# Mixing stage of a hybrid block kernel: a batch's sums from GpSimd to VectorE, and a new order of the work around them

## The chip, the cores and the metric

One Trainium2 chip, one core of it. The metric is the device time of one launch in microseconds; lower is better. All arithmetic is fp32, with a few bf16 helpers for ranks and biases.

## The reference

The input x has 8 batches of 1024 tokens with 128 features. Four blocks follow each other, each reading the layer-normalised x and adding its result to x:

```
x = x + attention(layernorm(x))      # linear attention, 16 heads of 8, rotary, relu features
x = x + ffn(layernorm(x))            # 8 experts, the best 2 of each token, weights val
x = x + mixing(layernorm(x))         # a recurrence over the 1024 tokens of a batch, per feature
x = x + ffn(layernorm(x))            # the same experts and router again
```

The expert block ends in `y[m] = val[m,0] * result[m,0] + val[m,1] * result[m,1]`. The mixing block forms keys, values and a gate from x and from x shifted by one token. Per feature it keeps a numerator and a denominator that decay by exp(w), with the exponents taken against a running maximum. Its output is sigmoid(r) times the quotient, through one more matrix.

## The kernel before, in words

The two expert stages gather tokens into queues by expert in DRAM. Each batch is half `c = 0` and half `c = 1`, of four tiles of 128 tokens. GpSimd scatters a batch's normalised rows into `queue_dram` by 16 indirect DMAs (`scatter`, L547 to L560), with a small memset of a scratch tile between two of them in all but the last batch (`space`, L545). The experts run over tiles of 256 rows, and scatter results into `result_dram`.

Between the two expert stages lies the mixing stage, the one that the diff touches. It runs once per batch b = 1 to 8, in program order on each engine (b = 2 to 5 in a loop). Each engine's part is called `mixing`. Work of several batches is in hand at once:

- Batch b itself: VectorE multiplies values with exponentials (`weighted_values`), runs two scans (`states`, L1558 and L1559), forms the outputs (`outputs`, L1564 to L1575) and the quotient (`divided`, L1582). TensorE multiplies with the output matrix on top of the old x (L1139, L1145), and ScalarE copies the sum to `xres` (L901). SyncE stores it.
- Batch b+1: ScalarE normalises its x into `hmix` (`normalise`, L655), with the reciprocal deviations (`inverse_deviations`, L649) and VectorE's `shift` (`scales_in`, L1245). TensorE turns it (L935) and forms the keys (L1114, L1115). VectorE takes the running maximum (`maxima`, L1543) and the differences to it (`gaps`, L1548). ScalarE clamps these (`clamp_past`, L836) and exponentiates (`exponentials`, L842 to L848), where L848 also needs TensorE's gate product.
- Batch b+2: the results of the first expert stage come back to `back_x` (tile name `qkv`). ScalarE multiplies them with the gates (`weight`, `weigh`, L753, 16 instructions). Then GpSimd adds, for each half, x and the first result (L611) and the second result (L613): `sums` and `combine`. VectorE takes the moments of the sum (`way_in_moments`, L1233 and L1238), which batch b+2 needs when it is normalised one batch later.
- Batch b-1 on its way to the second expert stage: it is normalised into `hffn`, routed by TensorE, and VectorE picks its experts (`choose`, L1276 to L1294) and its places in the queues (`place`, L1300 to L1309). `place_ready` starts the GpSimd scatter number b+7.

The order on VectorE in a batch is: `weighted_values`, both scans, the two shifts, `outputs`, `maxima`, `divided`, `gaps`, `choose`, moments of `xres`, `place`, moments of the sum of b+2. On ScalarE: the deviations of b-1 and of b+1 and the normalising, `invert` (L855, L859), `weight(b+2)`, `clamp_past(b+1)`, the two `xres` copies, `exponentials(b+1)`. On GpSimd, the sums of batch b+2 stand between scatter b+6 and scatter b+7, and wait in program order behind the scatter of the batch before. Batches 7 and 8 form no sums, and batch 8 looks at no next batch. After it come the scatters 14, 15 and 16, the plan of the second expert stage and that stage.

The sums of the batches 1 and 2 are made by VectorE already, inside the end of the first expert stage (L1367 and L1369, with the same tile shapes).

Of the kernel before, what the change touches and what calls it, by code (L numbers as in the profile page):

```python
# [66 lines left out]
def program(nc, x, cosine, sine, consts, w_qkv, w_out, g_qk, g_qk_swapped, g_out, bias_cols, w_router,  # L67
            router_rows, w_up, w_down, up_bias, down_bias, channel, w_k, w_v, w_r, w_o, out):
    with ExitStack() as ctx:
# [468 lines left out]
        def _(pool):  # L538
# [66 lines left out]
            def combine(c, b, s):  # L605

                pool.wait_ge(x_loaded[c], b * 16 + 16 * BATCH)
                pool.wait_ge(weighted[c], b)
                y = back_x[c].rearrange("p (j k) d -> p j k d", k=TOPK)
                total = xsum[s][c]  # L610
                nc.gpsimd.tensor_tensor(total[:], xin[c][:], y[:, :, 0, :], ALU.add).then_inc(first_added[c], 1)  # L611
                pool.wait_ge(first_added[c], b)
                nc.gpsimd.tensor_tensor(total[:], total[:], y[:, :, 1, :], ALU.add).then_inc(xsum_ready[c], 1)  # L613

            def sums(b, s):
                for c in range(HALVES):
                    pool.wait_ge(summed[c], b - 2)
                    pool.sem_inc(place_taken, 1)
                    combine(c, b, s)

            sums(3, 1)
            with pool.Fori(0, 2) as n:
                sums(n * 2 + 4, 0)
                scatter(n * 2 + (1 + BATCH), 1)
                sums(n * 2 + 5, 1)
                scatter(n * 2 + (2 + BATCH), 0)
            sums(BATCH, 0)
# [5 lines left out]
        def _(act):  # L633
# [122 lines left out]
            def weight(m):  # L756

                take_gates(m)
                for c in range(HALVES):
                    weigh(c, m)  # L760
                act.wait_ge(weighted[HALVES - 1], m)

# [58 lines left out]
            def normalise_in(b, s):  # L821

                for c in range(HALVES):
                    inverse_deviations(c, b + BATCH, var_ready, moment, rstd, rstd_ready)
                for c in range(HALVES):
                    normalise(c, scale_ready, b, xsum[s], rstd, shift, hmix, h_ready)
# [51 lines left out]
            def mixing(b, s, before, routed=True, ahead=True, weighed=True):  # L878
# [4 lines left out]

                if routed:
                    deviations_routed(b - 1)
# [8 lines left out]
                if weighed:  # L894
                    weight(b + 2)
                if ahead:
                    clamp_past(b + 1)
                for c in range(HALVES):
                    act.wait_ge(mixed_ready[c], b)
                    act.wait_ge(x_stored[c], (b + BATCH) * 16)  # L900
                    nc.scalar.activation(xres[c][:], tiles4(ps_half[c]), ACT.Copy).then_inc(xres_ready[c], 1)  # L901
                if ahead:
                    exponentials(b + 1)
# [8 lines left out]
            experts(FIRST)  # L912
            normalise_in(1, 1)
# [281 lines left out]
        def _(dve):  # L1195
# [359 lines left out]
            def states(row):  # L1555

                dve.wait_ge(ev_ready, row)
                return (mark(nc.vector.tensor_tensor_scan(num[:, after], expo[:, 2, :], ev, num[:, 0:1], ALU.mult, ALU.add)),  # L1558
                        mark(nc.vector.tensor_tensor_scan(den[:, after], expo[:, 2, :], expo[:, 3, :], den[:, 0:1], ALU.mult, ALU.add)))  # L1559
# [24 lines left out]
            def mixing(b, s, before, routed=True, ahead=True, two_ahead=True):  # L1584
# [3 lines left out]
                scans = states(b)  # L1588
                if routed:
                    scales_for_experts(b + (BATCH - 1))  # L1590
                if ahead:
                    scales_in(b + (1 + BATCH))
# [6 lines left out]
                if routed:  # L1599
                    choose(b + (BATCH - 1), SECOND, 1 - s, before)  # L1600
                for c in both:
                    dve.wait_ge(xres_ready[c], b + BATCH)
                moments(xres, stats2, moment2, var2_ready)
                if routed:
                    place(b + (BATCH - 1), SECOND, 1 - s)
# [135 lines left out]
```

## Time and profile before

| | |
|---|---|
| median of 3 runs | 1095.58 us (1095.22 to 1096.97) |
| the profiled execution | 1094.39 us |
| its span in the trace | 1092.5 us |
| mixing stage in it | about 545 to 857 us |
| busy in the span | PE 805.5, POOL 748.8, DVE 708.1, ACT 573.4 us |
| granted TensorE clock, mean | 0.839 |

PE is TensorE, DVE is VectorE, ACT is ScalarE, POOL is GpSimd and SP is SyncE. Times in the trace are microseconds from the start of the span. The mixing stage is read batch by batch: the first `hmix` instruction (L655) of a batch on ScalarE is used as the mark of that batch. In a row of the timeline several instructions of one line stand as one, with their number behind an x.

### The profile page before, as it was taken

What the parts mean: (1) busy time and instruction counts of PE and PEld (TensorE: products, weight loads), DVE (VectorE), ACT (ScalarE), POOL (GpSimd) and SP (SyncE); (2) the same over time, 40 slices, a digit from 0 to 9 for tenths busy, and PEclk for the clock granted to TensorE, in tenths of its full rate; (3) what the DMA queues carried; (4) which work ended last, traced back from release to release, by engine and by line L of the source; (5) the groups of instructions that cost most, each with busy time, mean ns of one, the idle gap of its engine ahead of it and who ended that gap; (6) DMA issues with size and microseconds to landing.
All of it is one profiled execution on the core that took longest, in us unless ns stands there. A gap on an engine that the chain in (4) does not pass through costs nothing.

```text
span 1092.5 us, 19253 instructions
## 1 busy us (share of the span) xinstructions
PE 805.5 (74%) x4480; PEld 648.4 (59%) x4481; DVE 708.1 (65%) x2600; ACT 573.4 (52%) x1588; POOL 748.8 (69%) x1091
## 2 busy tenths in 40 slices
PE   3687787876419999999855676555751399999991
PEld 2466667765408999998623344323441399999881
DVE  4588898885524454454568888888854155666665
ACT  2786676662204434335578888888840143433430
POOL 2007776675755888887802589898888388888884
PEclk9788887786559999999878887778855699999996
DMA  7023222222245565566312231331114355789885
GB/s 197 20 59 88 82 77 66 87 73 70 80 130 159 178 189 184 184 189 197 102 58 77 87 111 38 102 104 51 54 59 129 85 181 186 240 265 293 282 248 158
DMA packets 159975, 142.67 MB, mean 131 GB/s; under 512 B 17539, under 2 KB 132876, under 8 KB 159792
## 3 DMA queue, kind: packets, MB, share of 16 engines
q1 hardware_dynamic: 121744, 70.98, 23.5%
q10 hardware_dynamic: 20448, 37.23, 10.5%
q0 software_dynamic: 17728, 33.88, 9.0%
q8 instruction: 16, 0.26, 0.1%
q14 instruction: 39, 0.32, 0.1%
HBM read 93.47 MB, written 50.37 MB: 132 GB/s over the span
## 4 chain that ended last, share of the span: by engine, by line
PE 41%; POOL 17%; DVE 14%; ACT 12%; issue 11%; DMA 3%; DVEq 0%; POOLq 0%; SPq 0%; ACTq 0%; another core or an unknown queue 0%
PE banks L1059 14%; POOL queue_dram L557 8%; PE banks L1079 7%; POOL result_dram L570 6%; PE banks L935 4%; POOL spacer L545 3%; PE banks L961 3%; DVE stats L1233 3%; PE banks L949 2%; ACT hmix L655 2%; PE banks L1067 2%; PE banks L1114 2%; ACT qkv L753 2%; PE banks L989 2%; PE banks L1115 2%
## 5 line engine op out<-in xcount | busy, mean ns | idle before, releaser
L557 POOL DMA_INDIRECT queue_dram<-hffn,place_i x256 | 297.5, 1162 | 169.8 <-remote 119.4
L570 POOL DMA_INDIRECT result_dram<-ytile,result_row x284 | 280.6, 988 | 93.1 <-issue 39.6
L1059 PE MATMUL banks<-xt,tile_up 128*128 128x256 f32 x1136 | 271.8, 383 | 5.2 <-DVE gated L1412 5.2
L769 ACT ACTIVATE gated<-banks,tile_bias 128x256 f32<-128x256 f32 x284 | 119.0, 470 | 234.4 <-PE banks L1059 196.0
L1412 DVE SCALAR_TENSOR_TENSOR gated<-banks,tile_bias,gated 128x256 f32<-128x256 f32 x284 | 124.2, 479 | 157.1 <-ACT gated L769 156.4
L1059 PEld LDWEIGHTS banks<-xt,tile_up 128*128 128x128 f32 x1136 | 207.1, 192 | 28.8 <-issue 3.6
L1079 PE MATMUL banks<-wdown_sb,gated 128*128 x1136 | 149.9, 275 | 3.9 <-DVE ytile L1420 3.9
L1079 PEld LDWEIGHTS banks<-wdown_sb,gated 128*128 128x128 f32 x1136 | 138.2, 192 | 4.5 <-issue 4.3
L545 POOL MEMSET spacer<- 128x176 f32 x508 | 138.8, 273 | 0.2
L935 PE MATMUL banks<-k_sb,hmix 128*128 128x128 f32 x128 | 30.0, 380 | 98.7 <-ACT hmix L655 69.9
L1067 PE MATMUL banks<-k_sb,xtile 128*128 128x128 f32 x284 | 55.4, 277 | 55.5 <-DMA xtile<-queue_dram 55.5
L935 PEld LDWEIGHTS banks<-k_sb,hmix 128*128 128x128 f32 x128 | 19.9, 192 | 110.4 <-ACT hmix L655 86.9
L1067 PEld LDWEIGHTS banks<-k_sb,xtile 128*128 128x128 f32 x284 | 40.2, 143 | 70.5 <-issue 55.1
L775 ACT ACTIVATE xt<-banks 128x256 f32<-128x256 f32 x142 | 54.5, 384 | 52.0 <-PE banks L1067 51.9
L1401 DVE SCALAR_TENSOR_TENSOR result_row<-xtile,expert_all 128x2 int32<-128x2 f32 x142 | 30.2, 213 | 64.8 <-DMA xtile<-queue_dram 42.9
L961 PE MATMUL banks<-wqkv_sb,hmix_t 128*128 128x384 f32 x128 | 57.8, 536 | 7.9 <-DMA bias_rows<-split_dram 7.4
L1114 PE MATMUL banks<-hseq,wnow_sb 128*128 128x512 f32 x96 | 60.0, 711 | 0.3
L1420 DVE TENSOR_TENSOR ytile<-banks,down_bias_sb 128x256 f32<-128x256 f32 x142 | 58.6, 413 | 0.0
L1115 PE MATMUL banks<-hseq,wpast_sb 128*128 128x512 f32 x96 | 55.9, 668 | 0.0
L668 ACT ACTIVATE qkv<-banks 128x384 f32<-128x384 f32 x64 | 31.2, 490 | 31.4 <-PE banks L940 31.4
L935 PE MATMUL banks<-k_sb,hffn 128*128 128x128 f32 x128 | 22.3, 314 | 33.0 <-ACT hffn L655 17.7
L935 PEld LDWEIGHTS banks<-k_sb,hffn 128*128 128x128 f32 x128 | 18.0, 165 | 46.2 <-issue 17.5
(213 smaller groups left out, 1579.7 us busy)
## 6 DMA issues: line engine op xcount, KB each, us to landing
tile_up<-w_up ACTq DMA_DIRECT2D x142, 256.0 KB
xtile<-queue_dram SPq DMA_DIRECT2D x142, 130.0 KB, 2.3
qkv<-result_dram SPq DMA_DIRECT2D x24, 512.0 KB, 5.4
x_dram<-xres SPq DMA_DIRECT2D x32, 256.0 KB, 2.8
result_dram<-ytile,result_row POOLq DMA_INDIRECT x284
xin<-x SPq DMA_DIRECT2D x16, 256.0 KB, 4.5
xold<-x SPq DMA_DIRECT2D x16, 256.0 KB, 4.1
queue_dram<-hffn,place_i POOLq DMA_INDIRECT x256, 2.4
```

The lines of the kernel that those rows point to most:

```text
L545: clear = nc.gpsimd.memset(spacer[:, slot, :], 0.0)
L557: nc.gpsimd.indirect_dma_start(queue_dram, bass.IndirectOffsetOnAxis(ap=place_i[s][:, at:at + 1], axis=0), hffn[s][c][:, j, :], None).then ...
L570: nc.gpsimd.indirect_dma_start(result_dram, bass.IndirectOffsetOnAxis(ap=result_row[i % SLOTS][:, h:h + 1], axis=0), ytile[i % SLOTS][:, h ...
L769: last = nc.scalar.activation(gated[i % GSLOTS][:, h, :], ps_up[i % 2][:, h, :], ACT.Silu, bias=tile_bias[i % STEP][:, h:h + 1])
L935: last = nc.tensor.transpose(dst[:, j * P:(j + 1) * P], src[:, j, 0:D], ident)
L961: nc.tensor.matmul(dst, hmix_t[c][:, j * P:(j + 1) * P], wqkv_sb[:], start=True, stop=False)
L1059: last = nc.tensor.matmul(ps_up[i % 2][:, h, :], tile_up[i % WSLOTS][:, h * P:(h + 1) * P], xt[i % 2][:], start=True, stop=True)
L1067: last = nc.tensor.transpose(ps_xt[i % 2][:, part * P:(part + 1) * P], xtile[i % SLOTS][:, part, 0:D], ident)
L1079: last = nc.tensor.matmul(y, gated[i % GSLOTS][:, h, tokens], wdown_sb[:, bass.ds(e * (HCH * D) + h * D, D)], start=(h == 0), stop=(h == H ...
L1114: nc.tensor.matmul(part, wnow_sb[:, i, :], hseq[:, 1 + c * CHUNK:1 + (c + 1) * CHUNK], start=True, stop=False)
L1115: last = nc.tensor.matmul(part, wpast_sb[:, i, :], hseq[:, c * CHUNK:(c + 1) * CHUNK], start=False, stop=True)
L1412: last = nc.vector.scalar_tensor_tensor(gated[i % GSLOTS][:, h, :], ps_up[i % 2][:, HCH + h, :], tile_bias[i % STEP][:, HCH + h:HCH + h + ...
```

## The change

The sums of the batches 3 to 8 go from GpSimd to VectorE. GpSimd only scatters in the mixing stage. VectorE forms the sum of half 0 after `choose`, then `place` (which stood behind the moments of `xres`), then the moments of `xres`, then the sum of half 1, then its moments. On ScalarE the weighing is split: half 0 before the `xres` copies, half 1 after them, and `clamp_past` behind both. ScalarE computes the deviations of b+1 ahead of those of b-1. VectorE computes the shifts between the two scans, those of b+1 first, and not behind both.

```diff
@@ gpsimd
-            def combine(c, b, s):
-                pool.wait_ge(x_loaded[c], b * 16 + 16 * BATCH)
-                pool.wait_ge(weighted[c], b)
-                y = back_x[c].rearrange("p (j k) d -> p j k d", k=TOPK)
-                total = xsum[s][c]
-                nc.gpsimd.tensor_tensor(total[:], xin[c][:], y[:, :, 0, :], ALU.add).then_inc(first_added[c], 1)
-                pool.wait_ge(first_added[c], b)
-                nc.gpsimd.tensor_tensor(total[:], total[:], y[:, :, 1, :], ALU.add).then_inc(xsum_ready[c], 1)
-            def sums(b, s):
-                for c in range(HALVES):
-                    pool.wait_ge(summed[c], b - 2)
-                    pool.sem_inc(place_taken, 1)
-                    combine(c, b, s)
-            sums(3, 1)
             with pool.Fori(0, 2) as n:
-                sums(n * 2 + 4, 0)
                 scatter(n * 2 + (1 + BATCH), 1)
-                sums(n * 2 + 5, 1)
                 scatter(n * 2 + (2 + BATCH), 0)
-            sums(BATCH, 0)
             for b in range(BATCH - 3, BATCH + 1):
                 scatter(b + BATCH, b % 2, spread=b < BATCH)
@@ scalar
+            def deviations_in(b):
                 for c in range(HALVES):
                     inverse_deviations(c, b + BATCH, var_ready, moment, rstd, rstd_ready)
+            def normalise_in(b, s):
                 for c in range(HALVES):
                     normalise(c, scale_ready, b, xsum[s], rstd, shift, hmix, h_ready)
@@ scalar, mixing
+                if ahead:
+                    deviations_in(b + 1)
                 if routed:
                     deviations_routed(b - 1)
...
                 invert(b)
                 if weighed:
-                    weight(b + 2)
-                if ahead:
-                    clamp_past(b + 1)
+                    take_gates(b + 2)
+                    weigh(0, b + 2)
                 for c in range(HALVES):
                     act.wait_ge(mixed_ready[c], b)
                     act.wait_ge(x_stored[c], (b + BATCH) * 16)
                     nc.scalar.activation(xres[c][:], tiles4(ps_half[c]), ACT.Copy).then_inc(xres_ready[c], 1)
+                if weighed:
+                    weigh(1, b + 2)
+                    act.wait_ge(weighted[HALVES - 1], b + 2)
+                if ahead:
+                    clamp_past(b + 1)
@@ vector
-            def states(row):
+            def states(row, between):
                 dve.wait_ge(ev_ready, row)
-                return (mark(nc.vector.tensor_tensor_scan(num[:, after], expo[:, 2, :], ev, num[:, 0:1], ALU.mult, ALU.add)),
-                        mark(nc.vector.tensor_tensor_scan(den[:, after], expo[:, 2, :], expo[:, 3, :], den[:, 0:1], ALU.mult, ALU.add)))
+                num_done = mark(nc.vector.tensor_tensor_scan(num[:, after], expo[:, 2, :], ev, num[:, 0:1], ALU.mult, ALU.add))
+                between()
+                return num_done, mark(nc.vector.tensor_tensor_scan(den[:, after], expo[:, 2, :], expo[:, 3, :], den[:, 0:1], ALU.mult, ALU.add))
@@ vector, mixing
-                scans = states(b)
-                if routed:
-                    scales_for_experts(b + (BATCH - 1))
-                if ahead:
-                    scales_in(b + (1 + BATCH))
+                def shifts():
+                    if ahead:
+                        scales_in(b + (1 + BATCH))
+                    if routed:
+                        scales_for_experts(b + (BATCH - 1))
+                scans = states(b, shifts)
...
                 if routed:
                     choose(b + (BATCH - 1), SECOND, 1 - s, before)
+                def next_sum(c):
+                    if two_ahead:
+                        dve.wait_ge(summed[c], b)
+                        combine(c, b + 2, s)
+                next_sum(0)
+                if routed:
+                    place(b + (BATCH - 1), SECOND, 1 - s)
                 for c in both:
                     dve.wait_ge(xres_ready[c], b + BATCH)
                 moments(xres, stats2, moment2, var2_ready)
-                if routed:
-                    place(b + (BATCH - 1), SECOND, 1 - s)
+                next_sum(1)
                 if two_ahead:
                     way_in_moments(b + 2, s)
```

## Rows read from the trace of the kernel before

**Rows 1.** Chain of waits, 530 to 870: start, duration, what

```profile
715.02 1.23 POOL xmid L611
...
856.47 2.29 DMA queue_dram<-hffn,place_i
```

**Rows 2.** Timeline of POOL: start, duration, instruction, [idle before, releaser]; first issues of scatters

```profile
755.59 0.99 POOL L557 DMA_INDIRECT queue_dram<-hffn,place_i  x1 [0.86 <-remote]
...
786.05 0.96 POOL L557 DMA_INDIRECT queue_dram<-hffn,place_i  x1 [2.25 <-remote]
...
815.30 0.96 POOL L557 DMA_INDIRECT queue_dram<-hffn,place_i  x1 [0.17 <-POOL spacer L545]
...
837.52 0.96 POOL L557 DMA_INDIRECT queue_dram<-hffn,place_i  x1 [0.17 <-issue]
```

**Rows 3.** Windows, queue_dram instructions: stretch, length, POOL busy, PEclk, DMA share, GB/s

```profile
721.11:749.43 28.32, 21.74 (x16) 0.76 0.24 76
```

**Rows 4.** Waits of ACT, 600 to 770: us in total, times, longest

```profile
ACT hmix L655 <- DVE shift L1245: 8.8, 4, 2.6
```

**Rows 5.** Timeline of ACT: hmix, invert and the last exponential of batches

```profile
593.08 3.19 ACT L655 ACTIVATE hmix<-xmid,shift,rstd 128x128 f32<-128x128 f32 x8
...
622.79 1.02 ACT L848 ACTIVATE rope_s<-banks 128x1024 f32<-128x1024 f32 x1 [1.37 <-PE banks L1115]
...
626.03 3.19 ACT L655 ACTIVATE hmix<-xold,shift,rstd 128x128 f32<-128x128 f32 x8
...
693.84 3.19 ACT L655 ACTIVATE hmix<-xold,shift,rstd 128x128 f32<-128x128 f32 x8 [1.70 <-DVE shift L1245]
...
705.38 1.14 ACT L855 ACTIVATE rope_c<-rope_c 128x512 f32<-128x512 f32 x2
...
722.90 1.01 ACT L848 ACTIVATE rope_s<-banks 128x1024 f32<-128x1024 f32 x1
...
728.50 3.19 ACT L655 ACTIVATE hmix<-xmid,shift,rstd 128x128 f32<-128x128 f32 x8 [2.42 <-DVE shift L1245]
...
762.99 3.19 ACT L655 ACTIVATE hmix<-xold,shift,rstd 128x128 f32<-128x128 f32 x8 [2.59 <-DVE shift L1245]
```

**Rows 6.** Timeline of DVE: the sum of one half, as VectorE already makes it

```profile
531.84 0.68 DVE L1367 TENSOR_TENSOR xold<-xin,qkv 128x512 f32<-128x512 f32 x1
532.56 0.69 DVE L1369 TENSOR_TENSOR xold<-xold,qkv 128x512 f32<-128x512 f32 x1
```

**Rows 7.** Timeline of DVE in the mixing stage, batches 4 to 7

```profile
678.98 2.06 DVE L1293 COPY hffn<-top_f 128x4 f32<-128x4 f32 x2
...
704.46 2.35 DVE L1543 TENSOR_TENSOR_SCAN top<-w_sb,top,banks 128x1024 f32<-128x1024 f32 x1 [3.65 <-PE banks L1115]
...
742.68 1.22 DVE L1548 TENSOR_TENSOR rotated<-banks,top 128x1024 f32<-128x1024 f32 x1
...
758.16 2.35 DVE L1558 TENSOR_TENSOR_SCAN num<-expo,num,rotated 128x1024 f32<-128x1024 f32 x1
...
778.13 0.23 DVE L1276 COPY hffn<-k_sb 128x4 f32<-128x4 f32 x2
...
781.77 1.64 DVE L1233 BATCH_NORM_STATS2 stats<-xres 128x6 f32<-128x128 f32 x8
...
783.87 0.23 DVE L1300 TENSOR_REDUCE seen_new<-member 128x8 f32<-128x64 bf16 x1
```

**Rows 8.** Timeline of PE: last rank product of batch 7

```profile
781.85 0.19 PE L1000 MATMUL banks<-seen,ones_bf 128*128 128x64 bf16 x1
```

**Rows 9.** Timelines of ACT and PE in batch 1

```profile
572.23 4.78 ACT L753 ACTIVATE qkv<-qkv,gate 128x128 f32<-128x128 f32 x16
...
578.38 1.16 PE L1145 MATMUL banks<-wo_sb,squares 128*128 128x128 f32 x8 [0.52 <-DVE squares L1582]
...
582.72 1.28 ACT L842 ACT_TABLE_LOAD   x1
```

**Rows 10.** Timeline of PE: turning a batch's hmix after an idle time

```profile
627.73 1.12 PE L935 MATMUL banks<-k_sb,hmix 128*128 128x128 f32 x4 [4.98 <-ACT hmix L655]
```

More of the change, by code:

```diff
@@ L754, in weigh @@
                 last.then_inc(weighted[c], 1)
[L756 to L761, printed above, removed]
             def experts(f):
@@ L818, in experts @@
                 steps(LAST, FINAL)
-            def normalise_in(b, s):
+            def deviations_in(b):
                 for c in range(HALVES):
                     inverse_deviations(c, b + BATCH, var_ready, moment, rstd, rstd_ready)
+            def normalise_in(b, s):
                 for c in range(HALVES):
@@ L912, in _ @@
             experts(FIRST)
+            deviations_in(1)
             normalise_in(1, 1)
```

## The prediction

> **What bounds the kernel now.** I read the chain of waits of the mixing stage first, because it says who is late. In its later batches it goes from the end of a scatter to the sum on POOL (L611), to VectorE's moments and scans, and to `hmix` on ScalarE; from batch 7 on it is POOL's scatters alone up to 856.47, when the last one starts [rows 1]. So two things set the end of the stage: when scatter 14 can start, and the three scatters 14 to 16 that follow it without a gap. Scatter 14 starts at 786.05, after POOL has been idle for 2.25 us: it waits for its places, not for POOL. Scatter 15 follows at 815.30 and scatter 16 at 837.52, each directly behind the one before [rows 2]. Nothing behind scatter 14 gets shorter, so the change is worth what it brings forward place 14.
>
> The timeline of ScalarE gives the pace. The `hmix` marks of the batches 5 and 6 are 34.66 us apart (693.84 and 728.50) [rows 5]. In the later batches ScalarE idles before `hmix` for VectorE's shift and, between two batches, for nothing else of a size that the change touches; these waits are 8.8 us over four batches [rows 4]. POOL's own load is a scatter of 28.3 us [rows 3] plus the sums, four instructions of the kind that took 1.23 us [rows 1]: scatter 13 starts 34.5 us after scatter 12 (721.11 and 755.59) [rows 2, 3]. So POOL and the chain through ScalarE and VectorE are about level now, and the change must relieve both.
>
> **Batches 3 to 6, ScalarE's path.** One batch is 11.54 us from `hmix` to `invert` (693.84 to 705.38), 18.53 us from there to the end of the last exponential (722.90 plus 1.01), and then a table load and four small roots. This last part took 2.22 us where nothing waited (622.79 plus 1.02 to 626.03), and 4.59 us where the shift was late (723.91 to 728.50) [rows 5]. After the change the deviations of b+1 come first and their shift stands between the scans, so it is no longer behind the second scan, of 2.27 us. ScalarE's own work stays the same: the split of the weighing reorders it. The new period is 11.54 + 18.53 + 2.22 = 32.3 us. I take the four shift waits as gone but for 0.05 us each (the shift's round trip lies beside the two later roots): 8.8 - 0.2 = **8.6 us** [rows 4].
>
> **Does VectorE fit?** From `hmix` to `gaps` is 14.18 us (728.50 to 742.68). Then follow `gaps` 1.14, `choose` 3.64 (778.13 to 781.77, in batch 7, where no sum of POOL lies beside it), the sum of half 0, `place`, the moments of `xres` 2.10 (781.77 to 783.87), the sum of half 1 and its moments 2.10 [rows 5, 7]. A half's sum took 0.72 + 0.69 = 1.41 us on VectorE, with scatters running on POOL [rows 6]. That is the nearest row, with the same shapes. `place` took 1.4 us, bounded by its first instruction at 783.87 and the scatter's start at 786.05 [rows 2, 7]. Adding 1.2 us for `weighted_values`, 2.3 for the first scan and 0.3 for the shifts: 14.18 + 1.14 + 3.64 + 1.41 + 1.4 + 2.10 + 1.41 + 2.10 + 1.2 + 2.3 + 0.3 = 31.2 us. This is under 32.3, so ScalarE sets the period, with a slack of 1.1 us on VectorE. The 2.8 us that the sums add are mostly paid by what goes: in batch 4 two copies of 128x4 took 2.06 us together, just when POOL's sum began, where the two of L1276 take 0.23 [rows 7], and where VectorE waits for `xres` now, `xres` comes earlier, ahead of the second half's weighing and the clamps.
>
> The second scan starts about 1 us later than now, because VectorE waits for the roots of b-1 between the scans. The cover is the wait for the keys before the running maximum, 3.65 us in batch 5 [rows 7], of which the earlier `hmix` takes 2 and the later scan 1; some 0.7 is left. If that cover is gone, VectorE's path grows by what is over. Behind the new waits of VectorE on `weighted` and `summed` the queue holds `place` and the moments; half 0 is weighed some 3 us before VectorE comes to it. SyncE's stores and loads wait for `xres` and the sums, which come within 2 us of their present times, and the results they load are used more than 20 us later: nothing.
>
> **Batch 1** has no scatter and no shift wait. VectorE's quotient of the second half lay beside a sum on POOL, and the output product that needs it came after an idle 0.52 us, at 578.38. I take that idle time as gone: it ends at some 578.8. ScalarE has weighed half 0 by 574.6 (572.23 plus half of 4.78), so it now waits for that product where it had other work. It copies `xres` until 579.4, weighs half 1 in 2.4 and clamps in 2.1 us: the table load comes at 583.9 and not at 582.72 [rows 9]. That is **1.2 us lost**. **Batch 2** has a wait of 1.37 us of the last exponential for TensorE [rows 5], whose ranks and value products stand behind `choose`, itself beside POOL's sum in this batch. It goes: **1.4 us gained**.
>
> **Batch 7** forms no sums. `place` moves ahead of the moments of `xres`: it started at 783.87, and can start when the ranks are there, at 782.1 [rows 7, 8]. That is **1.75 us** for scatter 14. Scatter 13 must be done by then. Place 13 comes 14.18 + 1.14 + 3.64 + 1.41 + 1.4 = 21.8 us after the `hmix` of batch 6, its scatter 0.9 us later, and it runs 28.3 us: it ends 51.0 us after that mark. Scatter 14 can start 32.3 + 20.5 + 0.9 - 0.1, some 53 us after it. So POOL is free by 2 us.
>
> **Sum:** 8.6 - 1.2 + 1.4 + 1.75 = 10.5 us (rounded). The profiled execution took 1094.39 us and so becomes 1083.9; the median shown is 1.2 above it, so the forecast against it is 1095.58 - 10.5 = **1085.1 us**. A measurement of this kernel can tell about 0.2%, 2.2 us.
>
> **Unknown costs.** A half's sum on VectorE beside a scatter: at best as above, at worst each of its two instructions waits for one scatter issue of 0.96 to 0.99 us [rows 2]. I take the measured 1.41. What a sum does to the scatter: at best nothing, at worst four instructions stretch it by their own time and one restart each, 4 x (0.69 + 0.5) = 4.8 us. I take 0.7. TensorE's idle time before a batch shrinks by some 2 us: no cost, and see (d).
>
> **Rivals.**
> (a) *VectorE becomes the bound, half-way.* If each instruction of a sum loses 0.5 us, VectorE's path is 33.2 us. Four periods of 33.2 against the present 137.0 (626.03 to 762.99) [rows 5] gain 4.2; with about 1 us less in batch 2 and place, some 5 us in all are left: 1090.5. For: only 1.1 us of slack, and the added wait between the scans. Against: VectorE's instructions kept their time beside scatters [rows 6].
> (b) *VectorE's sums queue behind POOL's issues: slower.* Each of four instructions waits 0.96 us, 3.84 in a batch. VectorE's path is 35.0 us; the batches 3 to 6 take 140.2 and not 137.0, so 3.2 lost; batch 1 loses 1.2, batch 2 1.5, the earlier place gives 1.75: 4.1 us slower, 1099.7. The point from which it is slower is 0.75 us per instruction. For: rows 7 show a small copy held for 2 us by POOL. Against: that was POOL's sum, not a scatter.
> The Trainium skill, "SBUF — State Buffer", section "SBUF: two separate sides", says that whichever of VectorE and GpSimd takes their common port pair first holds it for the whole instruction while the other blocks, and that a VectorE instruction with two SBUF inputs competes only with a GpSimd one that reads SBUF. If an issue counted as one, its price would be that of (b).
> (c) *POOL stays the bound.* Scatters of 28.3 + 4.8 us follow each other at 33.3 us and not 34.3: 4 us gained before scatter 14, 1091.3. For: in the trace the issues stretch beside VectorE's work, 21.74 us for 16 [rows 3] against 15.4 at 0.96 each [rows 2]. Against: it needs 3.7 us from the sums.
> (d) *TensorE's clock stays up.* Turning `hmix` takes 1.12 us for four at the low level. If the shorter idle time kept it high, some 2 us more would go per batch, until scatters bind: 1079. Against: after 4.98 us of idle it was already low [rows 10].
> (e) *No effect:* a wait not seen here holds ScalarE before `hmix`: about 1095.
>
> **How the numbers follow.** Forecast 0.68, (a) 0.12, (b) 0.05, (c) 0.07, (d) 0.04, (e) 0.04. The forecast's own range is 1082 to 1088.5. The range reaches over (a) and up to (c): 1080.5 to 1091.5. Faster by over 0.2%: 0.91; within: 0.04; slower: 0.05.
>
> **What would show it.** Right: `hmix` marks 32 to 32.5 us apart in the batches 3 to 6; ScalarE's wait for the shift under 0.3 us; VectorE's sum instructions at 0.7 us; POOL idle 2 to 4 us before each scatter; scatter 14 at about 775.5; the three scatters behind it as long as now; batch 1 longer by about 1 us. Wrong: marks further apart with VectorE never idle (a, b), with POOL without gaps (c), or a scatter 14 that runs longer, because it starts at another point of VectorE's work.

## The result and the profile after

| | before | after |
|---|---|---|
| median | 1095.4 us (1092.88 to 1096.97, 4 runs) | 1079.77 us (1079.03 to 1080.33, 4 runs) |
| ratio | | 0.9861, 95% interval 0.9844 to 0.9877 |
| profiled execution, span | 1094.39, 1092.5 us | 1080.33, 1078.5 us |
| busy PE, POOL, DVE, ACT | 805.5, 748.8, 708.1, 573.4 us | 800.6, 715.5, 717.2, 573.1 us |

The kernel became faster, as forecast, but by 15.6 us and not by 10.5, which puts it 0.7 us below the range. Measured twice more, the changed kernel stood at 0.9887 (0.9865 to 0.9908) and 0.9867 (0.9851 to 0.9884) of the kernel before: 12.4 and 14.6 us, which would both lie inside the range. The size that follows from all three is about 14 us. That is also the difference of the two profiled spans, which the rest of this document takes apart.

The timeline of ScalarE after the change, marks of the batches 1 to 7 in the rows 562.30 to 750.63 (compare [rows 5]), and two waits for TensorE in between:

```profile
562.30 3.19 ACT L635 ACTIVATE hmix<-xold,shift,rstd 128x128 f32<-128x128 f32 x8
...
592.17 3.17 ACT L635 ACTIVATE hmix<-xmid,shift,rstd 128x128 f32<-128x128 f32 x8
...
623.90 3.17 ACT L635 ACTIVATE hmix<-xold,shift,rstd 128x128 f32<-128x128 f32 x8
...
631.89 0.60 ACT L641 ACTIVATE hffn_t<-banks 128x512 f32<-128x512 f32 x1 [0.76 <-PE banks L918]
...
655.13 3.17 ACT L635 ACTIVATE hmix<-xmid,shift,rstd 128x128 f32<-128x128 f32 x8
...
664.31 0.60 ACT L641 ACTIVATE hffn_t<-banks 128x512 f32<-128x512 f32 x1 [1.97 <-PE banks L918]
...
687.79 3.17 ACT L635 ACTIVATE hmix<-xold,shift,rstd 128x128 f32<-128x128 f32 x8
...
719.50 3.17 ACT L635 ACTIVATE hmix<-xmid,shift,rstd 128x128 f32<-128x128 f32 x8
...
750.63 3.17 ACT L635 ACTIVATE hmix<-xold,shift,rstd 128x128 f32<-128x128 f32 x8
```

No `hmix` row has an idle time before it any more. The stretch that a mark opens bears the number of its batch: 562.30 opens batch 1, 750.63 batch 7. The marks are 29.87, 31.73, 31.23, 32.66, 31.71 and 31.13 us apart.

VectorE: the sums of half 0 (642.36, 643.08) and of half 1 (647.21, 647.89) at their new places, and the waits that are left.

```profile
642.36 0.69 DVE L1350 TENSOR_TENSOR xmid<-xin,qkv 128x512 f32<-128x512 f32 x1
643.08 0.69 DVE L1352 TENSOR_TENSOR xmid<-xmid,qkv 128x512 f32<-128x512 f32 x1
...
647.21 0.65 DVE L1350 TENSOR_TENSOR xmid<-xin,qkv 128x512 f32<-128x512 f32 x1
647.89 0.69 DVE L1352 TENSOR_TENSOR xmid<-xmid,qkv 128x512 f32<-128x512 f32 x1
...
719.06 0.72 DVE L1228 SCALAR_TENSOR_TENSOR shift<-moment,rstd 128x4 f32<-128x4 f32 x4 [0.36 <-ACT rstd L629]
...
729.19 2.35 DVE L1526 TENSOR_TENSOR_SCAN top<-w_sb,top,banks 128x1024 f32<-128x1024 f32 x1 [0.23 <-PE banks L1098]
```

A sum takes what [rows 6] had said. Half 0 is summed here while POOL idles between two scatters, but for its last issue's end. Half 1 lies beside a scatter, and there it is POOL's issue that took longer than its 0.96 us, not the sum:

```profile
647.41 1.28 POOL L557 DMA_INDIRECT queue_dram<-hffn,place_i  x1 [0.16 <-issue]
```

The cover of the later second scan, 3.65 us in [rows 7], is down to 0.23 us here, and to 0.24 to 1.68 us in the batches 2 to 5.

POOL: first issues of the scatters 13 to 16 (compare [rows 2]).

```profile
741.38 0.97 POOL L557 DMA_INDIRECT queue_dram<-hffn,place_i  x1 [2.91 <-remote]
...
772.90 0.96 POOL L557 DMA_INDIRECT queue_dram<-hffn,place_i  x1 [4.70 <-remote]
...
800.86 0.97 POOL L557 DMA_INDIRECT queue_dram<-hffn,place_i  x1 [0.17 <-POOL spacer L545]
```

POOL idles before every scatter up to 14, and then issues without a gap to the last one at 842.05 (856.47 before [rows 1]). The stage ends as it did, only earlier.

| stretch, from row to row | forecast | found |
|---|---|---|
| up to the mark of batch 1 (562.79 and 562.30) | 0 | -0.49 |
| batch 1 (30.29 and 29.87) | +1.2 | -0.42 |
| batch 2 (32.95 and 31.73) | -1.4 | -1.22 |
| batches 3 to 6 (136.96 and 126.73) | -8.6 | -10.23 |
| last mark to scatter 14 (23.06 and 22.27) | -1.75 | -0.79 |
| scatter 14 (29.25 and 27.96) | 0 | -1.29 |
| scatters 15 and 16, to the last issue | 0 | +0.02 |
| behind it | 0 | +0.42 |
| sum | -10.55 | -14.0 |

### The profile page after: what moved, and what is told of

Read it like the earlier page. It is cut to its first block, busy times and chain, and to the rows that moved or that the text cites. A ratio compares the mean times of both kernels' runs of the same rounds, so it can differ in the third digit from the quotient of the medians.

```text
span 1078.5 us, 19231 instructions
## 1 busy us (share of the span) xinstructions
PE 800.6 (74%) x4480; PEld 647.3 (60%) x4481; DVE 717.2 (67%) x2624; ACT 573.1 (53%) x1588; POOL 715.5 (66%) x1067
## 4 chain that ended last, share of the span: by engine, by line
PE 44%; ACT 20%; POOL 10%; DVE 10%; issue 9%; DMA 4%; ACTq 1%; DVEq 0%; SPq 0%; POOLq 0%
PE banks L1042 16%; PE banks L1062 8%; POOL queue_dram L557 4%; PE banks L918 4%; POOL result_dram L570 4%; PE banks L944 3%; ACT qkv L733 3%; PE banks L932 2%; PE banks L1050 2%; DMA result_dram<-ytile,result_row 2%; PE banks L972 2%; ACT hmix L635 2%; POOL spacer L545 2%; PE banks L1097 2%; PE banks L951 1%
## 5 line engine op out<-in xcount | busy, mean ns | idle before, releaser
L545 POOL MEMSET spacer<- 128x176 f32 x508 | 134.1, 264 | 0.2
L1384 DVE SCALAR_TENSOR_TENSOR result_row<-xtile,expert_all 128x2 int32<-128x2 f32 x142 | 30.3, 213 | 67.4 <-DMA xtile<-queue_dram 43.0
L1097 PE MATMUL banks<-hseq,wnow_sb 128*128 128x512 f32 x96 | 57.8, 688 | 0.0
L1098 PE MATMUL banks<-hseq,wpast_sb 128*128 128x512 f32 x96 | 53.2, 638 | 0.0
```

The costliest lines, as they stand in the source:

```text
L545: clear = nc.gpsimd.memset(spacer[:, slot, :], 0.0)
L1097: nc.tensor.matmul(part, wnow_sb[:, i, :], hseq[:, 1 + c * CHUNK:1 + (c + 1) * CHUNK], start=True, stop=False)
```

## The experiments

Two theories stood against each other at first. A is the forecast's: both the order on ScalarE and VectorE and the load of GpSimd held the period. B: GpSimd alone did. "Changed kernel" is the kernel after the change. The runs came on four occasions. On the first the kernel before took a median of 1188.5 us; on the others 1096.0, 1096.0 and 1096.6. Ratios are to the kernel before on the same occasion. The changed kernel ran beside it on the second (e5) and the fourth (e15) alone, so what a single edit is worth is read against 0.9872, its mean over three measurements.

### One part alone, one part undone (e1 to e4, and e10 to e12)

**Sums only.** The kernel before, with the POOL sums removed and in VectorE's `mixing`:

```diff
                 if routed:
                     choose(b + (BATCH - 1), SECOND, 1 - s, before)
+                if two_ahead:
+                    for c in both:
+                        dve.wait_ge(summed[c], b)
+                        combine(c, b + 2, s)
                 for c in both:
                     dve.wait_ge(xres_ready[c], b + BATCH)
```

> The kernel before, with one part of the change: all four add instructions of a batch move from GpSimd to VectorE, behind the choice of experts; the weighing stays whole, the shifts stay behind both scans, the places behind the moments of xres. Theory A (the period was set by ScalarE's path with the shift wait, and only the new order takes that out): VectorE's path per batch is 14.2 + 1.1 + 3.6 + 2.8 + 2.1 + 1.4 + 2.1 + 1.2 + 4.5 + 0.3 = 33.3 us against 34.2 now; 3 to 5 us faster than before, about 1091. Theory B (GpSimd, which had to run a scatter and the sums one behind the other, set the period, and the rest of the change is decoration): nearly the whole gain, within 3 us of the changed kernel, 1080 to 1083.

e1: 1187.07 us, ratio 1.0025 (0.9984 to 1.0066). On that occasion VectorE had idle times of 1.2 to 2.7 us inside `choose`, between instructions of its own, and the marks of the batches 3 to 6 were 34.7 to 37.0 us apart. The same kernel on the third occasion is e10.

> The kernel of e1 once more: the kernel before with only the sums moved to VectorE, because e1 ran on a chip whose whole execution was 8% longer and had idle times of 1.2 and 1.5 us on VectorE with nothing to wait for. Theory A: marks 33.3 us apart, ScalarE's wait for the shift about 3.3 us in each batch from 3 on, 3 to 5 us faster than before, so a third of the gain. Theory B: nearly all of the gain. If e1 holds here too: no gain.

e10: 1090.68 us, ratio 0.9947 (0.9929 to 0.9964), 5.8 us faster than before. The waits of ScalarE, 585 to 790:

```profile
ACT hmix L635 <- DVE shift L1225: 7.5, 5, 1.8
```

The marks of the batches 2 to 6 are 33.2 to 34.0 us apart and the shift wait is still there, 1.5 us in each of these five. POOL now idles 3.1 to 7.2 us before each scatter from 10 to 14, and still most of the gain is missing: theory B falls. That the order is the missing part, as A says, is what e11 and e12 test.

**Shifts behind both scans** in the changed kernel:

```diff
                 num_done = mark(nc.vector.tensor_tensor_scan(num[:, after], expo[:, 2, :], ev, num[:, 0:1], ALU.mult, ALU.add))
-                between()
-                return num_done, mark(nc.vector.tensor_tensor_scan(den[:, after], expo[:, 2, :], expo[:, 3, :], den[:, 0:1], ALU.mult, ALU.add))
+                den_done = mark(nc.vector.tensor_tensor_scan(den[:, after], expo[:, 2, :], expo[:, 3, :], den[:, 0:1], ALU.mult, ALU.add))
+                between()
+                return num_done, den_done
```

> The changed kernel with the shifts back behind both scans. Theory A: the hmix of the next batch waits for the second scan again, the marks are 32.9 us apart instead of 31.7 on average, so 5 to 9 us slower than the changed kernel, 1085 to 1089, and ScalarE idles for the shift some 1.2 to 1.8 us per batch. Theory B: within 2 us of the changed kernel.

e2: 1177.69 us, ratio 0.9918 (0.9883 to 0.9953). The changed kernel did not run on that occasion, so what it lost was open.

> The kernel of e2 once more, the changed kernel with the shifts behind both scans, for the same reason. On the other chip ScalarE needed 3.3 to 3.8 us from its last exponential to hmix and not 2.07. Theory A: 1.3 to 1.7 us per batch here too, 7 to 10 us slower than the changed kernel. Theory B: within 2 us of it.

e11: 1091.21 us, ratio 0.9958 (0.9945 to 0.9971): some 9.4 us of the gain go with this one edit. The waits show the same 7.5 us as e10:

```profile
ACT hmix L635 <- DVE shift L1228: 7.5, 5, 1.8
```

They do not account for all of it. The batches 3 to 6 take 136.1 us and not 126.7. Of these 9.4 us, 6.4 lie between the last exponential and `hmix`. The other 3.0 lie between `hmix` and `invert`, which is 11.8 to 11.9 us in each of the four, where the changed kernel has 10.6 to 12.1.

**Weighing whole** again and `clamp_past` with it, ahead of the `xres` copies:

```diff
-                    weigh(0, b + 2)
+                    for c in range(HALVES):
+                        weigh(c, b + 2)
+                    act.wait_ge(weighted[HALVES - 1], b + 2)
+                if ahead:
+                    clamp_past(b + 1)
                 for c in range(HALVES):
                     act.wait_ge(mixed_ready[c], b)
...
-                if weighed:
-                    weigh(1, b + 2)
-                    act.wait_ge(weighted[HALVES - 1], b + 2)
-                if ahead:
-                    clamp_past(b + 1)
```

> The changed kernel with the weighing whole and, with the clamps, ahead of the xres copies again. The xres copies then end some 21.8 us after hmix, when VectorE has finished the first sum and the places and just comes to them. Theory A: ScalarE does the same work in another order and VectorE does not wait: within 1.5 us of the changed kernel, 1078 to 1082. Rival (the earlier xres is what lets VectorE run without idling): 1 us per batch, 5 to 7 us slower.

e3: 1171.14 us, ratio 0.9881 (0.9844 to 0.9917), on the first occasion alone. Batch 1 takes 29.91 us, and the batches 2 to 6 31.5 to 32.7 us, 160.5 us together where the changed kernel has 158.5. Splitting the weighing is worth at most some 0.4 us per batch; on an occasion with longer times than the others, this can't be told from nothing.

**Sums back on GpSimd** in the changed kernel: `combine` and `sums` as before the change on POOL, and `next_sum` empty on VectorE.

> The changed kernel with the sums back on GpSimd between the scatters. GpSimd then needs 28 + 5.2 + 0.2 = 33.4 us per batch against marks 31.7 us apart in the changed kernel. Theory A (both had to be relieved): GpSimd is the bound without gaps, 1.7 us per batch over four or five batches, 7 to 9 us slower than the changed kernel, 1087 to 1089. Theory B: all of the gain goes, 1093 to 1096. Small copies on VectorE beside GpSimd's sums take up to 2 us again.

e4: 1173.82 us, ratio 0.9903 (0.9866 to 0.994).

> The kernel of e4 once more, the changed kernel with the sums on GpSimd. Theory A: GpSimd needs 33.4 us per batch and sets the period from batch 4 on, 7 to 9 us slower than the changed kernel. Theory B: all of the gain goes.

e12: 1090.14 us, ratio 0.9940 (0.9926 to 0.9953), 7.5 us behind the changed kernel. POOL between the scatters 11 and 12, and VectorE in the same stretch:

```profile
713.93 0.96 POOL L557 DMA_INDIRECT queue_dram<-hffn,place_i  x1 [0.16 <-issue]
714.90 0.26 POOL L545 MEMSET spacer<- 128x176 f32 x1
715.11 1.28 POOL L611 TENSOR_TENSOR xmid<-xin,qkv 128x512 f32<-128x512 f32 x1
...
720.46 0.99 POOL L557 DMA_INDIRECT queue_dram<-hffn,place_i  x1 [0.16 <-issue]
```

```profile
720.40 1.65 DVE L1236 BATCH_NORM_STATS2 stats<-xmid 128x6 f32<-128x128 f32 x8 [5.95 <-POOL xmid L613]
```

POOL has no gap, VectorE idles 5.95 us for the sum, and the marks of the batches 5 and 6 are 34.2 us apart, near the 34.7 and 34.5 before the change (32.5 to 32.8 in the batches 2 to 4, where POOL was still catching up).

So the sums alone bring 5.8 us (e10) and the order alone 6.6 (e12), against 14.1 for both. By whole times the 12.4 us that the two add up to can't be told from the 14.1. The marks say more:

| | batches 3 to 6 | gain |
|---|---|---|
| kernel before | 136.96 us | |
| sums alone (e10) | 135.60 us | 1.4 |
| order alone (e12) | 133.84 us | 3.1 |
| both (changed kernel) | 126.73 us | 10.2 |

In these batches, where both limits act, each takes away one of two that lay at almost the same period, and one alone frees little. The rest of e10's gain lies elsewhere in its profile: 1.6 us in batch 1, 1.9 behind the last mark, and 2.2 ahead of batch 1, where nothing was changed.

The changed kernel's other details, that the deviations and shifts of b+1 come ahead of those of b-1, were not undone by themselves.

### TensorE's clock (e6, e9, e13)

> The changed kernel once more, unchanged, as the measure for the three kernels beside it on this chip. hmix marks of the batches 3 to 7 31.1 to 32.7 us apart, from the mark of batch 2 to the last scatter's start some 280 us, and 1.4% faster than before.

e5: 1082.82 us, ratio 0.9887 (0.9865 to 0.9908). Batch 1 took 30.86 us, 1 us more than in the first profile; all else lay within 0.6 us per batch.

Of the gain in the batches 3 to 6, 1.06 us lie between `hmix` and `invert` (45.49 us in all before, 44.43 after), and 1 us is lost there in batch 7. What ScalarE waits for in this part is the turned rows. Over 600 to 770 before the change these waits are longer in total than those for the shift [rows 4]:

```profile
ACT hffn_t L661 <- PE banks L935: 14.6, 10, 1.7
```

Windows of the changed kernel around the mark at 655.13, and one of the batch that the mark at 623.90 opens (stretch, length, busy times of PE, PEld, DVE, ACT and POOL, granted clock, DMA share, GB/s):

```profile
630.00:632.00 2.00, 2.00 (x8) 1.06 (x7) 2.00 (x2) 1.24 (x4) 2.00 (x2) 0.88 0.11 37
...
648.00:650.00 2.00, 0.00 (x0) 0.00 (x0) 1.90 (x8) 2.00 (x3) 1.83 (x3) 1.00 0.16 46
...
652.00:654.00 2.00, 0.00 (x0) 0.00 (x0) 1.97 (x2) 1.98 (x3) 1.83 (x3) 0.50 0.86 308
...
662.00:664.00 2.00, 2.00 (x6) 1.01 (x5) 1.97 (x3) 0.34 (x1) 1.83 (x3) 0.50 0.11 33
664.00:666.00 2.00, 2.00 (x6) 0.93 (x5) 0.59 (x1) 0.60 (x1) 1.83 (x3) 0.84 0.00 0
```

TensorE is idle for 9 us, and the clock is at its lower level (0.50 of full speed, 1.2 GHz) when `hmix` comes. Here it rises only at about 665, after the keys of half 0, some 10 us after `hmix`. In the batch with the wait of 0.76 us it rose in the window from 630, 6 to 8 us after `hmix`. So ScalarE's wait for the turned rows differs from batch to batch with the moment of that rise; whether the clock is the cause, the added products below tell. The differences are no noise: `hmix` to `invert` is 10.6 to 12.2 us in the batches 2 to 7 of all three profiles of the changed kernel, in the same order of short and long within 0.6 us.

e6 and e9 add products whose results nobody reads:

```diff
                     last.then_inc(r_ready, 1)
+                    for _ in range(10):
+                        nc.tensor.matmul(ps_turn3, ident, hseq[:, 1:1 + CHUNK], start=True, stop=True)
...
+                    if c and spare is not None:
+                        pe.wait_ge(gap_ready, spare)
+                        nc.tensor.matmul(bank[4], ident, k_sb[:, 0:CHUNK], start=True, stop=True)
                     if c:
                         pe.wait_ge(ht_ready[0], m)
                     turn(ps_turn3, hmix[c]).then_inc(h_turned[c], 1)
```

e6 has 8 in the first place and none in the second.

> The changed kernel with eight added 128x512 products of TensorE, whose results nobody reads, in its idle time ahead of the next batch's hmix (9 us of it). They tell what TensorE's clock is worth in ScalarE's path. Theory A (the clock's level after the idle time sets how long ScalarE waits from hmix to invert, and its scatter of 10.6 to 12.1 us is the term that my sum took from one batch): turning hmix takes 0.6 us for four and not 1.1, the keys of half 0 1.9 us and not up to 3.8, hmix to invert falls to 9 to 10 us in all batches, and the marks to 29.5 to 31 us apart, if the scatters of 28 us leave room: 6 to 12 us faster than the changed kernel. Theory B (the clock follows something else, or VectorE is the bound by then): marks as in the changed kernel, within 2 us of it.

e6: 1081.39 us, ratio 0.9864 (0.9843 to 0.9886), nothing gained over e5. The products ended 2.15 us before the first turning, and the clock still fell:

```profile
655.00:657.00 2.00, 0.63 (x2) 0.00 (x0) 1.87 (x6) 1.99 (x8) 1.83 (x3) 1.00 0.04 15
657.00:659.00 2.00, 0.66 (x4) 0.42 (x4) 2.00 (x2) 2.00 (x6) 2.00 (x1) 0.93 0.06 19
659.00:661.00 2.00, 1.10 (x5) 1.13 (x6) 2.00 (x3) 2.00 (x6) 1.83 (x3) 0.50 0.10 33
```

The first turning ran at the upper level (0.66 us for four and not 1.11), all behind it as without the products. This neither confirmed nor refuted that the clock sets the wait, so e9 fills the gaps too.

> The changed kernel with more added products than e6 (whose eight ended 2.15 us before hmix, and whose clock fell during the first turning and rose again at the same moment as without them): ten 128x512 products before a batch's hmix and one between the two turnings, results unread. Theory A: with no gap left the clock stays at the upper level, hmix to invert falls to 9.5 to 10 us, where VectorE's second scan and outputs end; VectorE then sets the period at about 30.5 us instead of 31.7: 4 to 8 us faster than the changed kernel. Theory B (the clock falls all the same): within 2 us.

e9: 1073.13 us, ratio 0.9795 (0.9777 to 0.9814), 8 us faster than the changed kernel. In the batches 3 to 7 the clock stayed at its upper level through the same part, and both turnings took 0.60 to 0.66 us:

```profile
655.00:657.00 2.00, 1.04 (x5) 0.50 (x4) 2.00 (x3) 2.00 (x6) 1.83 (x3) 1.00 0.09 31
657.00:659.00 2.00, 2.00 (x9) 1.06 (x8) 2.00 (x3) 2.00 (x6) 1.85 (x2) 1.00 0.01 2
```

`hmix` to `invert` is 9.6 to 9.7 us in every filled batch and the marks are 30.1 to 30.3 us apart. ScalarE's waits for the turned rows fell from 11.2 to 6.0 us over the batches 3 to 6, and the four batches from 126.7 to 121.0 us. VectorE then waits neither for the keys nor for the roots between the scans, so it is near its own limit. This version beats both kernels.

**The same products in the kernel before:**

> The kernel before with the same added products of TensorE as in e9. Theory A (GpSimd, which needs 28 + 5.2 us and waits for the places, holds the old order): hmix to invert falls to 9.7 us or less, but the sums still wait behind the scatters, so only batches 3 to 5 get shorter, and GpSimd fills the rest: 1 to 5 us faster than before. Theory B (the clock's part is independent of the order): 8 to 10 us faster than before, as between e5 and e9.

e13: 1095.48 us, ratio 0.9996 (0.9979 to 1.0013): nothing. In the batches 2 and 3 the products reached `hmix`, and it came to `invert` in 9.72 us too, 1.0 and 1.6 less than before. The mark behind batch 3 came as late as ever (660.10 before):

```profile
625.78 3.19 ACT L655 ACTIVATE hmix<-xold,shift,rstd 128x128 f32<-128x128 f32 x8 [1.50 <-DVE shift L1250]
635.50 1.14 ACT L855 ACTIVATE rope_c<-rope_c 128x512 f32<-128x512 f32 x2
...
660.31 2.03 ACT L655 ACTIVATE hmix<-xmid,shift,rstd 128x128 f32<-128x128 f32 x5 [4.12 <-DVE shift L1250]
```

The time saved stands as idle time before the next `hmix`, 4.12 us and not 2.06, because the sums on POOL and VectorE's chain behind them come no earlier: the last sum ends at 651.7, and the moments of it start at 651.80. In the batches 4 to 7 the products ended 1.9 to 4.3 us before the first turning, and by the second the clock was down (1.06 us for four and not 0.60). So the test is whole for the batches 2 and 3 alone.

### The end of the stage (e7, e8, e14)

The measure is from the last mark to the last scatter's issue: 91.42, 91.45 and 91.39 us in three profiles of the changed kernel.

**Places behind the moments of xres**, as before the change, in the changed kernel:

```diff
                 next_sum(0)
-                if routed:
-                    place(b + (BATCH - 1), SECOND, 1 - s)
                 for c in both:
                     dve.wait_ge(xres_ready[c], b + BATCH)
                 moments(xres, stats2, moment2, var2_ready)
+                if routed:
+                    place(b + (BATCH - 1), SECOND, 1 - s)
                 next_sum(1)
```

> The changed kernel with the places back behind the moments of xres. Theory A: in the batches 2 to 6 nothing changes, since GpSimd idles 3 to 5 us before each scatter; in batch 7 scatter 14 starts 2 us later and, running beside a later stretch of VectorE's work, is up to 1.3 us longer: 2 to 3.5 us slower than the changed kernel. Rival (the tail's length does not depend on it): within 1 us.

e7: 1081.67 us, ratio 0.9881 (0.9861 to 0.9901). The medians can't tell it from the changed kernel; the measure is 92.74 us. Scatter 14 started 1.8 us later after the mark, but took 27.47 and not 27.96 us. The place is worth 1.3 us at the end of the stage, and my guess that a later scatter 14 runs longer was wrong in sign.

**Scatter 15 bare**: `spread=b < BATCH - 1` in place of `spread=b < BATCH`.

> The changed kernel with scatter 15 without the 16 small memsets between its indirect DMAs, as scatter 16 already is. Between issues 1.26 us instead of 1.39: Theory A (the end of the stage is GpSimd's issuing alone): 2 us faster than the changed kernel. Rival (the memsets spread the DMA's load, without them rows land later): no gain, or a longer wait between the last issue and the first tile of the experts.

e8: 1080.34 us, ratio 0.9869 (0.9849 to 0.9890). The measure is 89.80 us, 1.6 less, which the medians can't tell. Scatter 15 took 20.6 us and not 22.2:

```profile
800.54 0.96 POOL L557 DMA_INDIRECT queue_dram<-hffn,place_i  x1 [0.17 <-issue]
801.81 0.96 POOL L557 DMA_INDIRECT queue_dram<-hffn,place_i  x1 [0.30 <-issue]
```

From the last issue to TensorE's first product with gathered rows it is 5.5 us, and 5.3 in the changed kernel. So the rows do not land later to speak of, and the rival falls.

**e9 with scatters 14 and 15 bare** (`spread=b < BATCH - 2`):

> The kernel of e9 with the scatters 14 and 15 without memsets between their indirect DMAs. In e8 a bare scatter 15 took 20.6 us and not 22.2. If the end of the stage is GpSimd's issuing alone, the two bare ones bring 3 to 4 us: 1069 to 1070 on a chip where the kernel before takes 1096. Rival: scatter 14 is held by VectorE's work and gains less than 1 us.

e14: 1071.75 us, ratio 0.9763 (0.9743 to 0.9783), the lowest of all. The measure is 87.25 us against 90.26 in e9: 3.0 us, the low end of what was expected if GpSimd's issuing alone sets the end of the stage. The median moved by 1.4 us and the intervals of e9 and e14 overlap, so the gain is shown in the profile alone.

> The changed kernel, as the measure for the two beside it: 1.1 to 1.6% faster than before.

e15: 1082.42 us, ratio 0.9867 (0.9851 to 0.9884); from mark to mark it is within 0.1 us of the first profile.

## Why the prediction was wrong in size

The mechanism was right and the sum was too small: 10.5 us against 14.0 in the profile. The step that failed is that the sum took away the waits that it could see and held everything beside them fixed. Three terms come of that: batch 1 (1.6 us), the batches 3 to 6 (1.6, of which 1.06 between `hmix` and `invert`) and scatter 14 (1.3, of which the change may be no cause at all). Place 14 went 1 us the other way, and small terms make up the rest. The other 1.6 us of the 15.6 are no term of the stage: they lie in which runs the medians came from, since two repeats gave 12.4 and 14.6.

- **What bounds the kernel: right.** Scatter 14 waited for its place, the scatters behind it kept their length (41.17 and 41.19 us from scatter 15 to the last issue), and the gain is what brought place 14 forward. e10, e11 and e12 show that both limits, POOL's load and the shift wait, had to go. The claim that they were about level is borne out by the batches 3 to 6: 1.4 and 3.1 us gained by either part alone, 10.2 by both.
- **Batches 3 to 6, 8.6 us: mechanism right, mis-sized by 1.6.** The stretch from the last exponential to `hmix` fell from 17.47 to 8.32 us over four batches, 9.15 and not 8.6: I had charged 2.22 us where 2.08 is what remains with the shift ready. The other 1.06 us is where the failed step shows best: the sum took `hmix` to `invert` as fixed at 11.54 us, one batch's value, and said that nothing else in ScalarE's waits was touched, though the waits for the turned rows were the largest of them in total. With the new order it is 10.6 to 12.1 us. It is set by when TensorE's clock rises, as the windows and e9 show. I had this as rival (d), but only as all or nothing, and gave it 4%.
- **Does VectorE fit: right.** From `hmix` to the next its path had a slack of 1.1 us on paper. In the trace VectorE waits for the roots between the scans by 0.29 to 0.48 us in four of the batches 2 to 6, so it was there first. A sum took 1.41 us per half or a little less. In e9, where VectorE has next to no wait left, the period is 30.3 us, and I had added up 31.2.
- **Batch 1, +1.2 us: the worst term, 1.6 us off.** POOL's sum had stretched VectorE's two quotients from 1.29 to 2.42 us together, which made `gaps` start later. I took half a microsecond of that as gone for the output product and nothing for `gaps`, though ScalarE's first clamp waited 2.54 us for it before the change:

```profile
579.55 1.15 ACT L836 ACTIVATE expo<-rotated,neg_w 128x1024 f32<-128x1024 f32 x1 [2.54 <-DVE rotated L1548]
```

In e10, with the sums alone moved, this wait is 0.92 us and batch 1 takes 28.67 us: 1.6 shorter. Of that, 1.16 is the stretch of the quotients, and 0.46 that the running maximum got its keys earlier. The new order then costs 1.2, but not by the mechanism that I named. VectorE idles 2.9 us between the scans for the roots, so `invert` comes 2.2 us later, and the output product is there when ScalarE wants it. The wait that I described exists in e11, where the shifts are behind: 2.87 us before the first `xres` copy, and batch 1 takes 31.02. It came in e5 too, in the changed kernel itself, with 0.46 and 0.30 us before the two copies.

- **Batch 2, 1.4 us: right** (1.22).
- **Place 14, 1.75 us: its part of 1.3 us is shown by e7**; in the profile 1 us of it was given back between `hmix` and `invert` in batch 7 (12.11 us, 11.10 before), the part that e9 shows to hang on the clock.
- **Scatter 14, taken as unchanged: 1.3 us shorter, and this may be luck.** All of the difference lies in issues beside VectorE's scans and outputs. Three took 2.54, 1.82 and 5.44 us before, and after the change five took 1.84 to 2.76. e13 keeps the order of the kernel before, its scatter 14 starts as late after the mark (23.03 and 23.06 us), and the same issues take this, where the kernel before has the one of 5.44 us:

```profile
792.65 5.44 POOL L557 DMA_INDIRECT queue_dram<-hffn,place_i  x1 [0.17 <-issue]
```

```profile
792.48 2.04 POOL L557 DMA_INDIRECT queue_dram<-hffn,place_i  x1 [0.17 <-issue]
...
794.94 1.85 POOL L557 DMA_INDIRECT queue_dram<-hffn,place_i  x1 [0.17 <-issue]
...
797.21 1.97 POOL L557 DMA_INDIRECT queue_dram<-hffn,place_i  x1 [0.16 <-issue]
```

So e13 has 27.86 us for scatter 14, as good as the changed kernel's 27.96, without the change. Over the profiles of the three later occasions it took 26.3 to 28.8 us. The kernel before was profiled once, so it stays open whether it takes 29.25 us as a rule; and so does the 0.5 us before the stage, since the mark of batch 1 lies anywhere from 560.5 to 564.7 in these profiles.

- **Rivals.** (a), (b) and (c) did not occur: VectorE's instructions kept their time, and POOL idled 2.9 to 4.7 us before each scatter from 10 to 14. No sum on VectorE was held; beside each sum of half 1 it was an issue that grew, to 1.3 or 1.4 us. For the restart of 0.5 us per instruction in (c) no row stood, and none was found.
- **The range** reached 4.6 us below the forecast and 6.4 above it, since its named rivals but one were slower ones. Three of the terms that I had left at zero gained instead: 0.5 us before the stage, 1.06 between `hmix` and `invert`, and 1.3 in scatter 14.

## What to carry to other kernels

When two limits lie at almost the same period, removing one shows little, and removing both shows more than the two single tests together (10.2 us against 1.4 and 3.1 in the batches 3 to 6): look for the second before judging the first, and compare the stretch where both act, since the whole time has other terms in it. A duration read from one batch of a loop is one sample; list it for all batches, since what varies (here the part behind an idle TensorE) is a term with a range of its own. So is a stretch that one profile alone has shown, as scatter 14's 5.44 us issue. And when work leaves an engine, list every instruction of the other engines that ran slower beside it, and who waits for each of them: they speed up too, as `gaps` did here, and not only where the engine itself was waited for.

## What was unexpected of the hardware

- Added TensorE work in an idle time made the kernel faster by 8 us (e9 against the changed kernel). A little less of it, ending 2.15 us before the first turning, did nothing (e6), and neither did the same work where another engine held the pace (e13).
- POOL's 128x512 adds beside two 128x512 multiplies of VectorE stretched these from 1.29 to 2.42 us together. VectorE's adds beside POOL's scatter issues kept 0.65 to 0.69 us, and the issues took 1.3 or 1.4 us in place of 0.96. Beside VectorE's scans and 128x1024 products, which kept some 2.35 and 1.2 us, single issues took up to 2.9 us after the change and up to 5.44 before it.
- On one occasion every kernel took 8% longer, the kernel before 1188.5 us, with most of it outside the mixing stage (e3: 283 us from the mark of batch 1 to the last scatter, 280 in the changed kernel elsewhere). For the two kernels with a part undone the ratio agreed within the intervals with the later one (e2 with e11, e4 with e12). For the sums alone it did not (e1 1.0025, 0.9984 to 1.0066; e10 0.9947, 0.9929 to 0.9964), and why stays open.
